# Weight-block sums of a Strassen kernel kept in DRAM after the first pass of each stage, and the identity added to W1 instead of W0

## Reference

```python
x = x + (einsum('bsd,od->bso', x, W0) + bias0 + einsum('bsr,bor->bso', einsum('bsd,brd->bsr', x, A0[id0]), B0[id0]))
x = x + (einsum('bti,oi->bto', x, W1) + bias1 + 2.0 * einsum('btr,bro->bto', einsum('bti,bir->btr', x, A1[id1]), B1[id1]))
```

## Time and profile before

| | |
|---|---|
| median of 3 runs | 2213.39 us (2213.34 to 2214.51) |
| the profiled execution's own time | 2214.27 us |
| its span, first to last instruction | 2212.5 us |
| PE busy | 2083.8 us (94%) |
| DVE busy | 1530.1 us (69%) |
| ACT busy | 725.5 us (33%) |
| POOL busy | 674.2 us (30%), 672.6 of it the 480 sums at L714 |
| DMA moved | 490.51 MB, queue share 72.8% of 16 engines |
| granted TensorE clock, mean | 0.981 |

### The profile page before, as it was taken

One profiled execution on the slowest core, in us unless ns is written; L12 is line 12 of the kernel. 1 busy time (PEld: TensorE's weight loads), 2 busy tenths in 40 slices (PEclk: granted clock), 3 DMA queues, 4 the chain that ended last, 5 costly groups with the idle time before them and its releaser, 6 DMA issues.

```text
span 2212.5 us, 27248 instructions
## 1 busy us (share of the span) xinstructions
PE 2083.8 (94%) x9196; PEld 1709.8 (77%) x9196; DVE 1530.1 (69%) x2128; ACT 725.5 (33%) x1264; POOL 674.2 (30%) x490
## 2 busy tenths in 40 slices
PE   3856999999999999999999999999999999999999
PEld 3745788777878787888777888877888777888887
DVE  2424677864777875677866777866777875867875
ACT  4632222322223233333333333333333323333332
POOL 0002140444131445230444221444322344312343
PEclk8977999999999999999999999999999999999999
DMA  7999885799674789564689564689554679654676
GB/s 217 363 282 326 255 245 165 242 294 318 195 207 117 222 267 315 149 190 124 213 252 317 158 188 124 215 248 303 180 173 134 209 231 313 197 160 145 200 221 195
DMA packets 355895, 490.51 MB, mean 222 GB/s; under 512 B 28972, under 2 KB 153900, under 8 KB 355372
## 3 DMA queue, kind: packets, MB, share of 16 engines
q1 hardware_dynamic: 355756, 488.77, 72.8%
HBM read 411.06 MB, written 77.60 MB: 221 GB/s over the span
## 4 chain that ended last, share of the span: by engine, by line
PE 66%; DMA 13%; DVE 8%; SPq 5%; issue 2%; POOL 2%; ACT 1%; POOLq 0%; DVEq 0%; ACTq 0%
PE acc L1244 20%; PE acc L1246 20%; PE acc L1245 20%; DMA w_second<-v_t 6%; DMA w_second<-wc_t 4%; DVE w_lo L877 3%; POOL w_raw L714 2%; PE h_acc L1175 2%; PE h_acc L1179 2%; DVE x_sum L889 1%; DVE c_out L1004 1%; DMA b_raw<-pb_t 1%; DMA hb_t<-e_raw 1%; SPq L456 1%; SPq L476 1%
## 5 line engine op out<-in xcount | busy, mean ns | idle before, releaser
L714 POOL TENSOR_TENSOR w_raw<-w_raw,w_second 128x512 f32<-128x512 f32 x480 | 672.6, 1403 | 1524.0 <-DMA w_second<-wc_t 886.9
L1244 PE MATMUL acc<-xop_hi,w_hi 128*128 128x512 f32 x2688 | 1055.7, 393 | 50.0 <-DVE w_lo L877 45.5
L1245 PE MATMUL acc<-xop_hi,w_lo 128*128 128x512 f32 x2688 | 1049.8, 391 | 0.0
L1246 PE MATMUL acc<-xop_lo,w_hi 128*128 128x512 f32 x2688 | 1049.6, 390 | 0.0
L877 DVE TENSOR_TENSOR w_lo<-w_raw,w_hi 128x512 fp32r<-128x512 f32 x672 | 567.7, 847 | 479.7 <-ACT w_hi L760 475.2
L760 ACT ACTIVATE w_hi<-w_raw 128x512 fp32r<-128x512 f32 x672 | 423.6, 631 | 1224.4 <-PE acc L1246 898.7
L1244 PEld LDWEIGHTS acc<-xop_hi,w_hi 128*128 128x128 f32 x2688 | 506.9, 189 | 174.1 <-DVE w_lo L877 65.4
L1246 PEld LDWEIGHTS acc<-xop_lo,w_hi 128*128 128x128 f32 x2688 | 506.7, 189 | 106.5
L1245 PEld LDWEIGHTS acc<-xop_hi,w_lo 128*128 128x128 f32 x2688 | 506.9, 189 | 103.7
L1004 DVE TENSOR_TENSOR c_out<-acc,c_out 128x512 f32<-128x512 f32 x352 | 233.4, 681 | 7.9 <-PE acc L1189 6.2
L889 DVE TENSOR_TENSOR x_sum<-x_in 128x512 f32<-128x512 f32 x240 | 230.4, 971 | 0.0
(11 more groups left out here) (99 smaller groups left out, 698.8 us busy)
## 6 DMA issues: line engine op xcount, KB each, us to landing
w_raw<-wc_t SPq DMA_DIRECT2D x448, 256.0 KB, 3.8
w_second<-wc_t SPq DMA_DIRECT2D x320, 256.0 KB, 4.9
w_raw<-v_t SPq DMA_DIRECT2D x224, 256.0 KB, 4.3
w_second<-v_t SPq DMA_DIRECT2D x160, 256.0 KB, 5.2
x_in<-x_t SPq DMA_DIRECT2D x128, 256.0 KB, 6.7
out_t<-c_out SPq DMA_DIRECT2D x128, 256.0 KB, 5.3
w_in<-w_t SPq DMA_DIRECT2D x16, 1024.0 KB, 7.8
v_t<-v_raw SPq DMA_DIRECT2D x16, 1024.0 KB, 8.3
```

Of the source, the lines that this page charges most:

```text
L714: nc.gpsimd.tensor_tensor(w_raw[:, r, :], w_raw[:, r, :], w_second[:, n % RAW2, :], ALU.add if sign > 0 else ALU.subtract).then_inc(w_summ ...
L1244: nc.tensor.matmul(bank[:, :], wh, xh, start=(k == 0), stop=False)
L1245: nc.tensor.matmul(bank[:, :], wl, xh, start=False, stop=False)
L1246: mm = nc.tensor.matmul(bank[:, :], wh, xl, start=False, stop=end)
```

## The change

1. **Sums kept.** `w_raw` and `w_second` become one buffer of 7 places. Passes 0 and 2 (`sums_w`) still load both blocks and sum on POOL, with the same rings of 4 and 3 places. ACT, before it splits such a tile, issues a DMA from its own queue that stores the sum to `ws_t`. The place is loaded again only when that store has landed (`wait_place`). Passes 1, 3, 4 and 5 load the sums from `ws_t`, one load per step, through all 7 places and 8 steps ahead instead of 6.
2. **I moved to W1.** `v_t` is now plain W0 transposed. DVE adds the identity to 16 tiles of W1 in `x_in` (`add_u_diagonal`) and subtracts it from 16 tiles of the result in `c_out` before they are stored. The additive term of passes 0 and 1 is `x_in`, so `load_c` and its 64 loads are gone. In the prologue the identity adds, the four `b0_rows` adds and the bias add go; one DVE instruction adds 2 x `a1_raw` to `ag` (`a1_added`).
3. **x loads.** Of the 32 x tiles of the next pass 24 are loaded in M7 and M6 (8 and 16, from step 2 of each) and 8, block (1,0), in M3 of their own pass. Before the first step block (0,0) is loaded where c tiles were, and `ag` is stored after it; the first eight steps load one x tile each.
4. **Order in the prologue.** `a0_raw` moves to the place of `b1_rows`, so its loads are issued at unit 10, behind a wait for the small stores. At its step 3 DVE waits until `ag` has been stored.

```diff
+    def sums_w(pl):
+        return pl in (0, PRE)
+    PLACES = RAW + RAW2
+    def place(s, second=False):
+        pl, r = divmod(s, STEPS * NPROD)
+        if not sums_w(pl):
+            return r % PLACES
+        return RAW + SUM_STEPS[s] % RAW2 if second else r % RAW
+    for s in range(NG):
+        at = s - (6 if sums_w(s // (STEPS * NPROD)) else 8)
+        LOAD_W_AT.append(max(at, LOAD_W_AT[-1] if s else 0, 0))
...
+            def wait_place(s, second):
+                if BEFORE[s, second] is None:
+                    return
+                s_old, second_old = BEFORE[s, second]
+                if second_old:
+                    sp.wait_ge(w_summed, SUM_STEPS[s_old + 1])
+                else:
+                    sp.wait_ge(w_lo_ready, s_old + 1)
+                    if is_sum_w(s_old):
+                        sp.wait_ge(w_stored[place(s_old)], STORED[s_old + 1][place(s_old)] * 16)
...
+                wait_place(s, False)
+                if two_blocks(s) and not sums_w(pl):
+                    src = ws_t[0 if pl < PRE else 1, i, j, :, :]
...
+                sp.dma_start(w_raw[:, place(s), :], src).then_inc(w_loaded[place(s)], 16)
+                if is_sum_w(s):
...
+                    sp.dma_start(w_raw[:, x, :], w_t[oh * MH + m, :, col:col + SW]).then_inc(w_loaded[x], 16)
...
             def w_split_hi(s):
                 if is_sum_w(s):
                     act_e.wait_ge(w_summed, SUM_STEPS[s + 1])
+                    act_e.dma_start(ws_t[0 if pl < PRE else 1, r // STEPS, r % STEPS, :, :], w_raw[:, x, :]
+                                    ).then_inc(w_stored[x], 16)
...
                 if t == Q_AFTER + 2:
...
+                if t == Q_AFTER + 3:
+                    sp.wait_ge(small_stored, 5 * 16)
                     for b in range(BATCH):
                         sp.dma_start(a0_raw[:, b, :, :], lora_a0[bass.ds(adapter_of(0, b), 1), :, :]
...
             for k in range(KH):
-                load_c(0, 0, 0, k)
+                load_x(0, 0, 0, k)
             sp.wait_ge(a0_copied, 1)
+            sp.wait_ge(a1_added, 1)
             sp.dma_start(ag_t.rearrange("b p n -> p b n"), ag[:, :, :, :].rearrange("p b k r -> p b (k r)")
                          ).then_inc(ag_stored, 16)
-            for k in range(KH):
-                load_c(0, 0, 1, k)
...
+                if pl + 1 < NPL and i == M7 and j >= 2 and (j % 2 == 0 or j == 15):
+                    load_x(pl + 1, 1, 1, (j - 1) // 2)
+                if pl + 1 < NPL and i == M6:
+                    for n in range(2 * KH):
+                        if j == 2 + n * 14 // 16:
+                            load_x(pl + 1, 0, 1 - n // KH, n % KH)
+                if pl > 0 and i == M3 and j % 2 == 0:
+                    load_x(pl, 1, 0, j // 2)
...
+            def add_u_diagonal(pl, th):
+                for t in range(TT):
+                    tile = x_in[:, block_no(pl, th), th * TT + t, t * P:(t + 1) * P]
+                    nc.vector.tensor_tensor(tile, tile, ident[:, :], ALU.add).then_inc(u_diag_added, 1)
...
+                    if pl < PRE and FINAL[blk] == (i, u) and oh == pl and m // TT == th:
+                        tile = c_out[:, b, m, m % TT * P:(m % TT + 1) * P]
+                        dve.wait_ge(c_updated, upd_count(q, m, u))
+                        nc.vector.tensor_tensor(tile, tile, ident[:, :], ALU.subtract).then_inc(c_diag_done, 1)
...
+                if g == 3:
+                    dve.wait_ge(t_copied, T_USES)
+                    dve.wait_ge(ag_stored, 16)
+                    dve.wait_ge(v_stored[1], NU // 2 * 16)
```

More of the change, by code:

```diff
@@ L163, in two_layer_lora_kernel @@
         SUM_STEPS.append(SUM_STEPS[-1] + is_sum_w(g))
+    PLACES = RAW + RAW2
[4 more added lines that the diff above has]
+        return RAW + SUM_STEPS[s] % RAW2 if second else r % RAW
+    TURN, BEFORE = {}, {}
+    held = [[] for _ in range(PLACES)]
+    for s in range(NG):
+        for second in (False, True)[:1 + is_sum_w(s)]:
+            here = held[place(s, second)]
+            TURN[s, second] = len(here)
+            BEFORE[s, second] = here[-1] if here else None
+            here.append((s, second))
+    STORED = [[0] * PLACES]
+    for s in range(NG):
+        STORED.append([n + (is_sum_w(s) and place(s) == x) for x, n in enumerate(STORED[-1])])
+    LOAD_W_AT = []
+    for s in range(NG):
+        at = s - (6 if sums_w(s // (STEPS * NPROD)) else 8)
+        LOAD_W_AT.append(max(at, LOAD_W_AT[-1] if s else 0, 0))
+    FIRST_LOADS = 4
     UNITS = [(mg, dg) for dg in range(GROUPS) for mg in range(GROUPS)]
@@ L210, in two_layer_lora_kernel @@
         xop_lo = sb("xop_lo", [P, XRING, T], f32r)
[L211 to L212 removed]
+        w_raw = sb("w_raw", [P, PLACES, SW])
         w_hi = sb("w_hi", [P, RING, KS, P], f32r)
@@ L316, in two_layer_lora_kernel @@
         x_loaded = [sem(f"x_loaded{b}") for b in range(4)]
-        c_loaded = [sem(f"c_loaded{b}") for b in range(4)]
+        u_diag_added = sem("u_diag_added")
         x_summed = sem("x_summed")
@@ L633, in _ @@
                 pl, i = divmod(q, NPROD)
-                s = g + 6
-                if g == 0:
-                    load_w(4)
-                    load_w(5)
-                if s < NG:
-                    load_w(s)
+                for s in range(FIRST_LOADS, NG):
+                    if LOAD_W_AT[s] == g:
+                        load_w(s)
                 if g < KH:
@@ L862, in _ @@
         def _(dve):
-            def add_diagonal(t):
-                mg, dg = UNITS[t]
-                for dl in range(4):
-                    tile = v_raw[:, t % 2, dl, dl * P:(dl + 1) * P]
-                    dve.wait_ge(t_copied, unit_use(t, dl) + 1)
-                    nc.vector.tensor_tensor(tile, tile, ident[:, :], ALU.add).then_inc(diag_added, 1)
             def split_unit_lo(t):
@@ L876, in w_split_lo @@
                 dve.wait_ge(w_hi_ready, s + 1)
-                nc.vector.tensor_tensor(flat(w_lo[:, s % RING, :, :]), w_raw[:, s % RAW, :],
+                nc.vector.tensor_tensor(flat(w_lo[:, s % RING, :, :]), w_raw[:, place(s), :],
                                         f(flat(w_hi[:, s % RING, :, :])), ALU.subtract).then_inc(w_lo_ready, 1)
@@ L1044, in _ @@
                 if t == Q_AFTER:
-                    for i in range(4):
-                        part = slice(i * T, (i + 1) * T)
-                        dve.wait_ge(t_copied, Q_USE + i + 1)
-                        nc.vector.tensor_tensor(q_rows[:, part], q_rows[:, part], b0_rows[:, part],
-                                                ALU.add).then_inc(q_ready, 1)
-                    dve.wait_ge(q_ready, 4)
+                    dve.wait_ge(t_copied, Q_USE + 4)
                     dve.wait_ge(b0t_stored, 6 * 16)
```

153 lines of the change are left out of this document (71 added, 82 removed).

## The result

| | before | after |
|---|---|---|
| median | 2213.36 us (2201.64 to 2214.51, 4 runs) | 2233.84 us (2231.87 to 2234.9, 4 runs) |
| profiled execution, its span | 2214.27, 2212.5 us | 2231.87, 2230.1 us |
| DMA moved | 490.51 MB | 431.74 MB |

The ratio is 1.0098, with a 95% interval of 1.007 to 1.0126: slower by 1%. I had forecast 2205.5, faster. Every sum that was to go is gone and 59 MB are moved less, and yet the kernel is 20 us slower. First the page of the changed kernel: engines (busy us, share, instructions), two groups (busy us, mean ns of one, idle time before), three kinds of DMA (KB each, median us to landing).

The account below looks back on a forecast made before the run. PE's matmul spacing (1959 us fixed) was taken to set the pace nearly everywhere, with losses where DMA engines are full. -29 + 15 + 7 - 1 = -8 us gave 2206.3 for the profiled execution, 2205.5 for a median run; range 2180 to 2236.

Parts of the forecast that it names:

- the pair: M7 with M6 of passes 0 and 2, where stores are added: +10 us in pass 0, +11 in pass 2.
- The gain of passes 1, 3, 4 and 5: Passes that load stored sums: -11, -9.5, -8.5 in passes 1, 3, 4 and 0 in pass 5, together -29 us.
- Step 4: Start of pass 0: with c tiles gone its 13.6 us wait shortens; it comes 5 us earlier (bounds 0 and 10).
- 28.1 MB x 1.21 = 34 MB take 110 us at that, 113 with a few gaps left: M7 with M6 of pass 2: DMA bytes at 310 GB/s for a full share, against 100.8 us before; taken as +11.
- the loop through the store: Passes 0 and 2: reloading after the store takes 10.7 us against 10.9 for 4 steps; light products +1 and +2 us.
- the second rival: The store sets the pace: M7 and M6 lose 20 us more in passes 0 and 2; total 2236; chance 0.25.
- the first rival: The new stores fit: M7 and M6 of passes 0 and 2 lose nothing more; total 2183; chance 0.20.
- the loop at near-full engines: 0: Pass 0, steps 4 to 15: as many transfers as before for eight steps, then fewer; no net cost, 0.
- The prologue: Before the first step: v store earlier, a0 loads later behind the small stores; -1 us (bounds -6 and +7).
- the third rival: The prologue eats it: a0 loads wait for late small stores, first step 8 us later, total within 0.2%; chance 0.05.
- The identity: Passes 0 and 1: sixteen adds and sixteen subtractions, under 12 us of DVE, hidden beside matmuls: 0.
- my case: The main forecast, whole kernel: -8 us, 2205.5 for a median run, own range 2193 to 2217; chance 0.50.

Follow-up runs that it names:

- run 3: Changed kernel, stores' bytes sent from a constant tile so no place waits for them; later passes load the first weight block instead: 2202.9 us, ratio 0.9951.
- run 1: Changed kernel without its 160 stores of sums and the waits for them; later passes load the first weight block instead: 2176.71 us, ratio 0.9826.
- run 2: Changed kernel with sums made in every pass and nothing stored; identity, x-load and prologue changes stay: 2197.04 us, ratio 0.9919.
- runs 8, 9: Small-stores wait, a0 and h_bias loads later: in the changed kernel 2232.22 us (1.0091); in the one summing every pass, storing nothing, 2193.6 us (0.9923).
- run 7: Changed kernel without the 16 subtractions of the identity from the composite matrix in passes 0 and 1: 2227.55 us, ratio 1.0066.
- run 5: Changed kernel with ACT issuing the store of a sum after the split to w_hi instead of before it: 2229.14 us, ratio 1.0086.

## Why the prediction was wrong

**Term by term.** In the span -8 was forecast and +17.6 measured, 25.6 us apart. 7.1 of them are the start (-1 against +6.1), 10.8 pass 0 (+7 against +17.8: M2 took 5.7 and M1 4.7 more than before), 7.6 pass 2 (+15 against +22.6: the pair +16.8 where I had 11, M1 +3.4), 0.1 the other passes.

**Right.** The gain of passes 1, 3, 4 and 5: -29 forecast, -28.9 measured. (By pass it was -11, -9.5, -8.5 and 0 against -8.3, -12.9, -9.9 and +2.2; w_lo now runs three steps ahead where the marks between those passes lie, not two, which moves some 2.7 us from one side of a mark to the other.) Step 4 was to wait 8 or 9 us instead of 13.63:

```profile
204.78 0.79 PE L1305 MATMUL acc<-xop_hi,w_hi 128*128 128x512 f32 x1 [8.27 <-DVE w_lo L919]
```

And w_lo without POOL beside it, in pass 3, 0.69 us as in the earlier trace rows (beside POOL the longest before was 1.82 us, not the 1.50 that I had read; no term rests on it):

```profile
L919 DVE TENSOR_TENSOR w_lo<-w_raw,w_hi 128x512 fp32r<-128x512 f32 x113 | 78.0, 691 | 109.5 <-ACT w_hi L809 109.0
```

**Right in its own terms, but not the bound.** "28.1 MB x 1.21 = 34 MB take 110 us at that, 113 with a few gaps left": with the bytes and without the wait the pair in pass 2 took 111.1 us at 305 GB/s and a share of 0.99 (run 3), where I had 310 for a full share. That run is nearest to what my sum describes, and its 2202.9 us are near the 2205.5 of the forecast, in part by luck: its start came 5.6 us later than before, M2 of pass 0 was 4.9 us longer and M5 of pass 0 9.4 shorter. In M7 with M6 of pass 0 +10 was forecast and +9.9 measured after, by luck, since that is 20.2 us of bytes and wait less 10.3 for the x and c loads (89.5 in run 1). The 425 GB/s of "HBM Reference" in the Trainium skill, section Specifications (TRN2), were not seen over any product. The most there is 346 GB/s, in M5 of pass 0 of run 3, at a share of 1.09 (323 after, 324 before). In the prologue, where transfers have 0.5 and 1 MB and not 256 KB, the changed kernel came near that figure for 7 us, with loads and stores mixed:

```profile
100.00:107.00 7.00, 6.62 (x46) 5.76 (x44) 3.39 (x2) 4.12 (x6) 0.00 (x0) 1.00 1.05 413
```

**The step that failed: the loop through the store.** I wrote "it just fits, if the store is as fast as an output store", took +1 and +2 for the light products, and left the loop out of M7 and M6. The price of the stores is 57 us, half of it the wait. The point from which it decides was given rightly: landings of load and store above 8.9 us together. I counted 4.0 + 4.7 from M1 of pass 2 before. After, load and store took 5.3 + 4.8 in that very product, since the store's own bytes load the engines (the same load took 4.3 in run 1), and 5.9 + 5.7 in M7: above 8.9 in every sum product of passes 0 and 2 but M2 of pass 0 (4.6 + 4.2). What was said against the rival, that the store is alone on ACT's queue, is worth 1.5 us of a landing (5.7 against 7.2 of `out_t` in the same window), where 5 were needed. Compared product by product with run 1, the stores cost M7 and M6 20.2 us in pass 0 and 19.8 in pass 2, M1 4.2 and 4.4, and M5 of pass 0 7.6. So the mechanism of the second rival happened, with its direction; its 2236 against 2233.8 is close in part by accident, as its start and its M5 were not these. I had given it 0.25, and 0.50 to a case that needed the loop to fit with 0.2 us to spare, on landings measured before the stores were there. That reading alone should have turned the two round.

The Trainium skill's "DMA: Bandwidth & Descriptors", section Anatomy of one DMA, spoke for the first rival: its fit, made for DMAs of GpSimd, gives 2.6 us for 256 KB. In the four passes without stores the loads of `ws_t` did land in 2.7 us, the median of 320; in the sum products of passes 0 and 2 the same size took 4.2 to 7.2. So the trace bears the figure out on lightly loaded engines alone, and the turn went over full ones.

**M5 of pass 0.** "the loop at near-full engines: 0" for steps 4 to 15 was wrong: 64.1 us without stores (run 2), 71.5 with them, 75.6 before. With the c loads gone and the x loads moved M5 gained 11.5 us, twice my 5 (step 4's shorter wait is 5.4 of them; which transfers gave the rest was not tried), and the stores took 7.4 of it back.

**The prologue.** -1 forecast, +6.1 measured, inside the bounds of -6 and +7. The small stores landed at 128.5, later than both cases that I had worked out (117 and 126): the third rival's own premise, "as late as `hb_t` did, 129". Whether this cost the total anything is open: taking the wait away started the first step 9.8 us earlier and changed no total (runs 8, 9).

**The identity.** "under 12 us of DVE in two passes of 340 and more, hidden": hidden by the pass, not at the place where the subtractions stand, the end of M3 of pass 0, where PE waited 4.7 us (1.1 before, 1.7 in run 7) and M2 got 5 us longer.

**Range and signs.** 2233.8 lies in the range of 2180 to 2236. A DMA share of 0.97 or more, which I had named as the sign of my case, did not come: 0.91. The first w_lo moved by 6.1 us, just over the 6 that I had named as a sign of being wrong. The sign of the second rival came: SP waits 271.1 us for the stores, 55.1 of them in a pair of products that takes 117.6, and M1 of pass 2 takes 49.4 us. Of its two parts only the first can tell: "light products above 45" held before too (M1 of pass 2 took 46.0).

## What to carry to other kernels

When a buffer is to be stored before it is loaded again, add up one turn of its place, landings included, and divide it by the steps that it carries; take the landings of the fullest stretch, with the new transfers in it, not of a light one. Here, where the turn was longer than its four steps, the wait cost about as much as the bytes; moving the issue in ACT's program changed nothing, and leaving the stores out of the full stretches helped (more places were not tried). And a saving spread over stretches that have slack (here 320 loads and sums in passes that lost 10 us each) must be weighed against a cost that falls on the stretches that have none.

## What the runs showed of the hardware

- A DMA that stands behind an activation in ACT's program did not wait for the activation's end: all 160 issues left before it, 149 within 0.02 us after the activation's start and 11 ahead of that start, as the one shown, 0.04 us after the sum (run 5).
- A store of 64 KB landed in 5.2 us where 256 KB landed in 5.7 (share 0.85 and 0.91). Both have 128 rows, of 512 B and 2 KB: in this full stretch the bytes of a transfer hardly set its landing.
- The last of the small stores, `hb_t`, 0.5 KB, landed 26.0 us after its issue (24.8 before). The 1 MB tile issued ahead of the small stores had landed at 106.8, so it was not that one; the small stores are 3 MB together, and the 1 MB tiles issued behind them at 103.75 and 106.27 landed after 26.6 us each. Between 112 and 117 us the share was 0.90 at 121 GB/s. Why was not tried.
